# Attention with eight-wide heads: masks by sixteen 32x32 tiles, and work passed from VectorE to GpSimd

## What is computed

```python
x = x + _L0_xattn_ref(_layernorm(x), ctx, ctx, ...)      # 16 heads of width 8, band mask
x = x + _L0_ffn_ref(...);  x = x + _L1_xattn_ref(...);  x = x + _L1_ffn_ref(...)
x = x + _L2_xattn_ref(_layernorm(x), ctx, ctx, mask, ...) # 16 heads of width 8, mask from an input
x = x + _L2_ffn_ref(...);  x = x + _L3_xattn_ref(...);  x = x + _L3_ffn_ref(...)
```

```python
q = proj(query, W_q, b_q); k = proj(key, W_k, b_k); v = proj(value, W_v, b_v)   # 16 heads of 8
scores = einsum('bhqd,bhkd->bhqk', q, k) / sqrt(8)
scores = where(mask, scores, finfo.min)
attn = softmax(scores, axis=-1)
out = einsum('bhqk,bhkd->bhqd', attn, v) @ W_o.T + b_o
```

## Time and profile before

| | us |
|---|---|
| median of 3 runs | 1926.64 |
| lowest run | 1926.18 |
| the profiled execution, its own time | 1944.06 |
| its span, first to last instruction | 1942.5 |
| mean granted TensorE clock in it | 0.922 of full speed |

### The profile page before, as it was taken

One profiled execution on the slowest core, in us unless ns is written; L12 is line 12 of the kernel. 1 busy time (PEld: TensorE's weight loads), 2 busy tenths in 40 slices (PEclk: granted clock), 3 DMA queues, 4 the chain that ended last, 5 costly groups with the idle time before them and its releaser, 6 DMA issues.

```text
span 1942.5 us, 48480 instructions
## 1 busy us (share of the span) xinstructions
PE 1696.6 (87%) x18886; PEld 1241.8 (64%) x18886; DVE 1086.4 (56%) x3147; ACT 887.7 (46%) x2432; POOL 652.9 (34%) x656
## 2 busy tenths in 40 slices
PE   6999974897599999989999827996899999999978
PEld 3666663775478878865666617996466666666753
DVE  6777665685522221126687734555466655665558
ACT  3444311685145444333433305664455556555525
POOL 3332103684211111113335363553132333333315
PEclk9999966887599999999999958998899999999969
DMA  5000001000000000016400011223100000000001
GB/s 183 9 14 8 3 1 32 18 7 1 6 1 2 1 2 1 2 59 250 178 15 24 23 40 52 59 58 96 39 18 2 17 18 17 7 1 1 2 1 44
DMA packets 48828, 63.55 MB, mean 33 GB/s; under 512 B 8106, under 2 KB 37701, under 8 KB 48349
## 3 DMA queue, kind: packets, MB, share of 16 engines
q1 hardware_dynamic: 44253, 51.98, 8.2%
q0 software_dynamic: 4352, 8.47, 1.4%
HBM read 32.29 MB, written 28.65 MB: 31 GB/s over the span
## 4 chain that ended last, share of the span: by engine, by line
PE 57%; issue 9%; DVE 9%; POOLq 3%; POOL 3%; DVEq 2%; ACT 1%; DMA 1%; SPq 1%; PEldq 0%; PEld 0%; ACTq 0%
PE single L1852 5%; PE quad L1840 5%; PE single L2173 3%; PE quad L2156 3%; PE single L652 2%; PE quad L2162 2%; PE pair L1813 2%; PE pair L2536 2%; PE single L2520 2%; PE quad L2571 2%; PE quad L156 1%; PE quad L2562 1%; PE single L2548 1%; PE single L2571 1%; PE pair L1896 1%
## 5 line engine op out<-in xcount | busy, mean ns | idle before, releaser
L2774 POOL TENSOR_TENSOR arena<-arena 128x512 f32<-128x512 f32 x128 | 130.4, 1039 | 297.9 <-DVE arena L2693 297.9
L263 POOL TENSOR_TENSOR rstd<-var_eps,neg_half 128x4 f32<-128x4 f32 (+1 forms) x64 | 66.5, 1039 | 315.0 <-DVE var_eps L259 261.0
L1925 ACT ACTIVATE arena<-quad,arena 128x256 f32<-128x256 f32 x256 | 110.9, 475 | 99.8 <-PE quad L1840 99.7
L909 POOL TENSOR_SCALAR arena<-arena 128x512 f32<-128x512 f32 x56 | 86.7, 1564 | 176.0 <-ACT arena L711 176.0
L2016 DVE TENSOR_TENSOR arena<-single,arena 128x512 f32<-128x512 f32 x32 | 22.1, 692 | 208.1 <-PE single L1852 208.1
L757 ACT ACTIVATE arena<-quad 128x1024 f32<-128x1024 f32 x86 | 86.3, 1023 | 105.7 <-PE pair L636 54.1
L2629 ACT ACTIVATE arena<-pair,arena 128x128 f32<-128x128 f32 x256 | 90.9, 380 | 89.0 <-DVE arena L2688 89.0
L2629 ACT ACTIVATE arena<-quad,arena 128x128 f32<-128x128 f32 x256 | 90.9, 381 | 86.4 <-DVE arena L2688 86.4
L1840 PE MATMUL quad<-arena,wide 128*128 128x256 f32 x512 | 123.3, 389 | 2.8 <-issue 1.9
L1852 PE MATMUL single<-wide,arena 128*64 128x128 f32 x2048 | 123.9, 275 | 0.0
L1852 PEld LDWEIGHTS single<-wide,arena 128*64 128x64 f32 x2048 | 110.7, 137 | 15.7 <-issue 10.0
(11 more groups left out here) (518 smaller groups left out, 4558.4 us busy)
## 6 DMA issues: line engine op xcount, KB each, us to landing
tokens_by_expert<-arena SPq DMA_DIRECT2D x22, 780.0 KB, 8.9
arena<-in_ctxT SPq DMA_DIRECT2D x32, 256.0 KB, 2.9
arena<-tokens_by_expert SPq DMA_DIRECT2D x72, 65.0 KB, 1.8
wide<-in_w SPq DMA_DIRECT2D x2, 2048.0 KB, 10.6
arena<-outputs_by_choice SPq DMA_DIRECT2D x16, 256.0 KB, 3.9
wide<-in_wgu SPq DMA_DIRECT2D x1, 2736.0 KB
x<-in_x SPq DMA_DIRECT2D x4, 512.0 KB, 7.3
out_x<-x SPq DMA_DIRECT2D x8, 256.0 KB, 2.3
```

The lines of the kernel that those rows point to most:

```text
L909: mm = pool.tensor_scalar(kv[g % 2][:, :, a, :], kf[g % 2], kmask[:, a:a + 1], None, ALU.mult)
L1925: act.activation(h1T[e % 4][:, f, :], bank[2 + f][:, 0:G * K], ACT.Gelu_apprx_tanh, bias=b1c[:, e, f:f + 1]).then_inc(s["h_evac"], 1)
L2774: pool.tensor_tensor(part, part, inv[t % 3][:, 4 * r:4 * r + 4].unsqueeze(2).broadcast_to([P, 4, P]), ALU.mult).then_inc(s["norm_ready"], 1)
```

## The change

It has five parts, all in `small_heads` and what feeds it.

1. **Masks.** `mask_strips` takes the place of `mask_banks` in layers 0 and 2. A set is sixteen matmuls with a 32x32 identity, eight for strips 0 and 1 ahead of the second wait and eight for strips 2 and 3 behind it. Bank r is fed by row strip r. The mask is held in four copies, turned by 0, 32, 64 and 96 partitions. For layer 0 ScalarE makes three of them by twelve copies of 32x128 (`band_turns`) before it waits for the weights, and TensorE waits once for `band_turned`. For layer 2 they come by 14 DMAs where there were 6, and VectorE converts eight tiles, one per block from n = 7 to 14, where it converted four at n = 7.
2. **Maxima.** `split_max` for blocks 2 to 31 goes from VectorE to GpSimd, as a cast and a subtraction without the sign, which goes into `chooser` instead. VectorE's `maximum` waits for the split of two blocks before.
3. **Rows.** In layer 0 `normed(g)` for g >= 2 goes from VectorE at j = 1 to GpSimd at j = 2.
4. **Keys.** `masked` runs in two pieces of two multiplications, at j = 0 and j = 1.
5. **Order on GpSimd.** In layer 0 its list goes by blocks. `later_consts` stands at n = 11.

```diff
+        def mask_strips(pe, strips, banks, turns):
+            for c in range(4):
+                for r, bank_r in zip(strips, banks):
+                    rows = slice(32 * r, 32 * r + 32)
+                    pe.matmul(bank_r[32 * c:32 * c + 32, :], identb[rows, rows],
+                              turns[(c - r) % 4][rows, :].unsqueeze(1).broadcast_to([32, 4, P]), start=True,
+                              stop=False, skip_group_check=True)
...
-                    mask_banks(pe, [bank_of(m, 0), bank_of(m, 1)], mask_bias[l]["S"])
+                    if m == 0 and l == 0:
+                        pe.wait_ge(s["band_turned"], 1)
+                    mask_strips(pe, (0, 1), [bank_of(m, 0), bank_of(m, 1)], mask_turns[l]["S"])
                     if m == 0:
                         pe.wait_ge(s["k_evac"], 2)
...
-                    mask_banks(pe, [bank_of(m, 2), bank_of(m, 3)], mask_bias[l]["S"])
+                    mask_strips(pe, (2, 3), [bank_of(m, 2), bank_of(m, 3)], mask_turns[l]["S"])
...
-                    mask_banks(pe, [bank_of(n, 0), bank_of(n, 1)], mask_bias[l]["T"])
+                    mask_strips(pe, (0, 1), [bank_of(n, 0), bank_of(n, 1)], mask_turns[l]["T"])
                     pe.wait_ge(s["s_free"], min(2 * n + 3, 2 * N))
-                    mask_banks(pe, [bank_of(n, 2), bank_of(n, 3)], mask_bias[l]["T"])
+                    mask_strips(pe, (2, 3), [bank_of(n, 2), bank_of(n, 3)], mask_turns[l]["T"])
...
+        def band_turns(act):
+            turns = mask_turns[0]["S"]
+            for k in range(1, 4):
+                for r in range(4):
+                    f = (r + k) % 4
+                    mm = act.activation(turns[k][32 * r:32 * r + 32, :], turns[0][32 * f:32 * f + 32, :], ACT.Copy)
+            return mm
...
+                act.wait_ge(consts_in, 1)
+                if l == 0:
+                    band_turns(act).then_inc(s["band_turned"], 1)
                 act.wait_ge(w_in[l], 16 * w_loads[l])
-                act.wait_ge(consts_in, 1)
                 act.wait_ge(cols_in, 1)
...
+            def split_max(eng, m):
+                eng.drain()
+                wide_mx = mx[m % 2].rearrange("p (r a) -> p r a", r=4)
+                lanes = mhl[m % 2].rearrange("p (r c) -> p r c", r=4)
+                eng.tensor_copy(lanes[:, :, 0:4], wide_mx)
+                eng.drain()
+                eng.tensor_tensor(lanes[:, :, 4:8], wide_mx, lanes[:, :, 0:4], ALU.subtract).then_inc(s["mhl_ready"], 1)
...
                 def maximum(m, p):
                     dve.wait_ge(s["s_ready"], m + 1)
+                    if m >= 2 and p == 0:
+                        dve.wait_ge(s["mhl_ready"], m - 1)
...
                     if n + 2 < N:
                         for p in range(2):
                             maximum(n + 2, p)
-                        split_max(n + 2)
...
+                def split(m):
+                    pool.wait_ge(s["s_free"], 2 * m + 2)
+                    split_max(pool, m)
...
                 if l == 0:
-                    for g in range(NG):
-                        if g + 2 < NG:
+                    for n in range(N):
+                        g, j = divmod(n, G)
+                        if j < 2 and 2 <= g + 1 < NG:
+                            masked(g + 1, (2 * j, 2 * j + 1))
+                        if j == 1 and g + 2 < NG:
                             first_rstd(pool, g + 2)
-                        if g == 2:
+                        if j == 2 and g + 2 < NG:
+                            pool.wait_ge(s["tr_ready"], g + 1)
+                            pool.drain()
+                            normed(pool, g + 2)
+                        if j == 3 and g >= 1:
+                            if g >= 2:
+                                residual(g)
+                            pool.wait_ge(s["stats_ready"], g)
+                            rstd_of(pool, (g - 1) * G)
+                        if n == 11:
                             later_consts(pool)
...
+                        if n + 2 < N:
+                            split(n + 2)
...
                 else:
                     for n in range(N):
                         g, j = divmod(n, G)
-                        if j == 0 and 2 <= g + 1 < NG:
-                            masked(g + 1)
+                        if j < 2 and 2 <= g + 1 < NG:
+                            masked(g + 1, (2 * j, 2 * j + 1))
...
+                        if n + 2 < N:
+                            split(n + 2)
                         if n >= 16:
```

113 lines of the change are left out of this document (49 added, 64 removed).

## The result

The changed kernel takes 1936.05 us (median of 6 runs, 1929.08 to 1937.68), the kernel before 1927.49 (6 runs on the same occasions). One of those six took 2845.06 us, in a slow state, and is left out of the ratio. The ratio is 1.0042, with an interval of 1.0030 to 1.0053: a little slower, outside the range of the prediction and on the other side. By the 2% measure it is no change. The profiled execution took 1937.68 us with a span of 1936.0.

A forecast was written before the change was run, and what follows sets the result against it. TensorE was taken to set the pace in the two attentions of width 8. Terms -10.6 + 0.8 - 2.5 - 1.0 = -13.3 us took the median 1926.64 to 1913.3 us; parts' bounds 1905 to 1921, with rivals 1900 to 1931.

The forecast's parts named there:

- GpSimd's order, "I cost it at nothing": GpSimd's queue in the attention blocks: it reaches the wait for the next maxima in time, 0.4 us left, costing nothing.
- GpSimd is late: Rival, chance 0.1: at 2.5 us per split, layer 2's split slips 1.3 us in six to eight blocks; 1921 us.
- the rival on stages between: Rival, chance 0.15: stages running between 2.4 and 1.2 GHz shift in time, 8 us either way; 1905 or 1921.
- Masks, -10.6 + 0.8: Mask sets: 0.18 us saved in each of 59, 10.6 us in all; 0.8 us lost in 62 blocks of `turned`.
- too many streams: Rival, chance 0.1: only two of four moving streams per row strip run at a time in the masks; 1938.8 us.
- eight tiles at a time: Rival, chance 0.05: only eight mask tiles run at a time, so nothing is saved at `scores`; 1923.9 us.
- Split off VectorE, -2.5: Layer 2 blocks where VectorE's reduction is late: one split less saves 0.5 us in each of five, 2.5 us.
- The split on GpSimd, 0.8 us: Cast and subtraction of the maxima on GpSimd: 0.8 us per split, upper bound 2.5, with 2.46 us left until needed.
- not 0.55, within its bounds: Layer 0's `normed` on GpSimd: about 0.55 us each, between 0.4 and 1.56, hidden and costed at nothing.
- The start, -1.0: Kernel start: earlier table load starts TensorE 1.28 us earlier, of which 1.0 us is gained; bounds 0.2 to 1.28.
- The forecast's -13.3: Whole kernel: sum of the forecast's terms, 13.3 us saved, giving 1913.3 us from the median of 1926.64.

The follow-up runs named there:

- e1: The changed kernel with layer 2's power on GpSimd moved to j = 2, ahead of the split of that block; 1921.71 us, ratio 0.9972.
- e7: e1 plus two unread products in TensorE's pause between the first and second scores of each attention; 1916.71 us, ratio 0.9954.
- e5: The kernel before, unchanged, profiled a second time; 1925.70 us in one execution.
- e11: e9 with the masks of both score steps laid by eight 64x64 products again; 1922.37 us, ratio 0.9978.
- e9: The changed kernel with layer 2's power before the split, blank fills sent one at a time and two unread products in TensorE's starting pauses; 1911.06 us, ratio 0.9921.
- e10: e9 with the split of every later set of maxima back on VectorE; 1916.74 us, ratio 0.9943.
- e4: The changed kernel with only the split of the maxima back on VectorE; 1923.54 us, ratio 0.9982.

## Why the prediction was wrong

- *GpSimd's order, "I cost it at nothing".* This step failed, and it is the largest part of the miss. It asked whether the split is in time for its reader, TensorE's transpose, and it is. The power was only counted as load ahead of the split (4.2 us in its block); that the split is also ahead of the power, with a wait for VectorE in it, and that VectorE's `rows_normal` reads the power one block later, was not asked. In its place the runs show a power eight us late, VectorE standing up to 4.81 us for it, and 10 to 11.5 us lost in five blocks (14.3 between the medians of after and e1).
- *The rival "GpSimd is late"* had the engine but not the place or the size: it gave 1921 and watched the transpose. The waits of L538 for VectorE (94.4 us) say that GpSimd had time there.
- *Clock at the start.* "Full clock" was read in the earlier trace rows and taken for given. The pause between the first and the second `scores` was in the trace of before, and with the change the clock falls in it: 4.4 us in layer 0 and 2.9 in layer 2 (e7 gives both back). No term and no rival had it; the rival on stages between looked at other stages, which moved by 0.6 and 0.7 us from e5 to after.
- *Masks, -10.6 + 0.8.* Right as far as they go: 0.19 us per set for 0.18, 0.34 to L661. Layer 0 gave 5.6 us. In layer 2 all of the 5.8 went in stops of TensorE beside the fills (3.7 in e1), a cost that no term and no rival had; with these paced, e11 against e9 gives 9.6 us in the attentions, 10.6 with e9's stop. The rivals of too many streams and of eight tiles at a time are refuted by the block above: all sixteen go in one round.
- *Split off VectorE, -2.5.* Right in size: e10 against e9 has 2.2 us in the late blocks without the stop. In the changed kernel 1.3 us of it shows in blocks 14, 29 and 30 (against e4); in blocks 21 and 22 the late power is mixed in.
- *The split on GpSimd, 0.8 us.* Right: 0.56 us from the start of the cast to the end of the subtraction (97.40 to 97.96), some 0.9 with the 0.33 of idle ahead of it where nothing is waited for (1018.40 to 1019.31). GpSimd's two ops last 0.20 and 0.22 us where VectorE's lasted 0.17 each, so the factor of two did not show on ops this small. `normed` there is 0.80 us each, not 0.55, within its bounds and hidden. From the groups of 40 to 230 us (busy, mean ns, idle before):

```profile
L546 POOL TENSOR_SCALAR arena<-x,mean,rstd 128x128 f32<-128x128 f32 x24 | 18.9, 797 | 1.2 <-issue 1.2
...
L540 POOL TENSOR_TENSOR arena<-arena 128x16 bf16<-128x16 f32 x28 | 6.3, 224 | 4.3 <-issue 0.7
L538 POOL CAST arena<-arena 128x16 bf16<-128x16 f32 x28 | 5.5, 198 | 94.4 <-DVE arena L811 94.4
```

- *The start, -1.0.* Wrong, it gave nothing. The answer to the earlier trace rows:

```profile
0.79 1.28 ACT L243 ACT_TABLE_LOAD   x1 [0.79 <-PEq L2932]
3.25 3.81 ACT L243 ACTIVATE maskS0by<-maskS0by 32x128 bf16<-32x128 bf16 x12 [1.18 <-POOLq L235]
9.84 0.40 ACT L776 ACTIVATE arena<-ident,acol 128x128 f32<-128x128 f32 x1 [2.77 <-DVE acol L295]
10.38 0.76 PE L695 MATMUL single<-wo,arena 128*128 128x128 f32 x2 [10.38 <-ACT arena L776]
16.71 1.40 DVE L546 TENSOR_SCALAR arena<-x,mean,rstd 128x128 f32<-128x128 f32 x4
18.17 0.42 PEld L591 LDWEIGHTS single<-ident,arena 128*128 128x128 f32 x4 [0.25 <-DVE arena L546]
```

The table and the copies are out of the way by 7.1 us, as reckoned. But ScalarE then waits for VectorE's `acol`, so TensorE gains 0.74 us for 1.28, and the second `turn` (18.17 for 18.30) hangs on VectorE's rows, which end at 18.11 for the 17.25 taken from before: VectorE's list begins 0.56 us later (9.67 for 9.11), and the rows take 1.40 for 1.11 beside GpSimd's `masked` at 16.97.

Added up, the parts about close the account. The forecast's -13.3 without the start's 1.0 is -12.3. The blocks of the late power (+11.5), those of the stops (+5.8) and the clock at both starts (+7.3) make it +12.3, and between the profiles of e5 and after it is +11.8.

## What to carry to other kernels

When a wait moves to another engine, follow everything behind it in that engine's list to its own reader, one block on, and not only the moved work to its reader; the cure here is the same code one block earlier. Look for pauses of TensorE at a stage's start before shortening work ahead of them, since a change that saves time elsewhere can bring the lower clock there, and two unread products in the pause can hold it. When an edit puts more instructions on TensorE, look at what the DMA engines do meanwhile. The fastest version is e9, 1911.06 us.

## What was not expected of the hardware

- TensorE stopped for 1.31 us (e1) and 2.14 us (after) within a group of masks while the fills had the DMA engines full, and not in that place with the fills one at a time. The Trainium skill (Runtime: NRT & Kernel Launch, Instruction fetch mechanics) says that the sequencer fetches its next block of instructions by a DMA queue of its own while it executes, and calls the cost mostly hidden. The size agrees with the page's 16 KiB (16384 bytes in each of the 164 packets). That it stays hidden does not hold beside the fills: 3.7 us in four blocks of e1. All 29 stops end 1.25 to 1.57 us after such a packet landed.
- Sixteen 512-column bf16 products on 32x32 tiles run in one round, 0.37 us from the first to the next kind, with no more than 0.03 us between the starts of the two halves.
- The same pause of TensorE (busy 1.46 of 4 us) brought up to 13.7 us at 1.2 GHz in one kernel and none in another, and in single profiles what told them apart was as small as the size of the mask products or a start 0.8 us earlier. Filling it gave e7 back 5.2 us of e1's time to the third block in layer 0, and 3.3 us in layer 2's first two blocks.
